# One Trainium2 core, an AdaLN block: the attention product in three fp32r parts, and two steps of VectorE in another order

## What is computed

```python
h = _layernorm(x, axis=-1) * (1 + ca) + sa
# attention
qkv = h @ w_qkv + b_qkv                      # q, k, v: 8 heads of 64
scores = einsum('bhld,bhle->bhde', q, k) / sqrt(64)
attn = softmax(scores, axis=-1)              # 64 x 64 per head
out = einsum('bhld,bhde->bhle', v, attn)     # joined over heads
out = out @ w_fc + b_fc + h
x = x + ga * (_layernorm(out) * gamma + beta)
# channel mix
h = _layernorm(x, axis=-1) * (1 + cb) + sb
h_prev = shift(h, 1)                         # the token before
r = sigmoid((mu_r * h + (1 - mu_r) * h_prev) @ W_r.T)
k = square(relu((mu_k * h + (1 - mu_k) * h_prev) @ W_k.T))
x = x + gb * (r * (k @ W_v.T))
```

## Time and profile before

| | |
|---|---|
| time, median of 3 runs | 690.93 us (690.6 to 691.36) |
| time of the profiled execution | 690.6 us |
| its span | 688.9 us |
| PE busy | 670.7 us (97%) |
| DVE busy | 561.0 us (81%) |
| ACT busy | 393.8 us (57%) |
| POOL busy | 317.5 us (46%) |

### The profile page before, as it was taken

One profiled execution on the slowest core, in us unless ns is written; L12 is line 12 of the kernel. 1 busy time (PEld: TensorE's weight loads), 2 busy tenths in 40 slices (PEclk: granted clock), 3 DMA queues, 4 the chain that ended last, 5 costly groups with the idle time before them and its releaser, 6 DMA issues.

```text
span 688.9 us, 11754 instructions
## 1 busy us (share of the span) xinstructions
PE 670.7 (97%) x3712; PEld 539.4 (78%) x3712; DVE 561.0 (81%) x1254; ACT 393.8 (57%) x871; POOL 317.5 (46%) x520
## 2 busy tenths in 40 slices
PE   7988999999999999999999999999999999999896
PEld 6777886888778887879868887788878788687674
DVE  5693999789887998889887898979988898658973
ACT  1424575566754675474855667546754747547662
POOL 5272864573254642565335742646325753214320
PEclk9989999999999999999999999999999999999999
DMA  8849345485836666572855849366665528628225
GB/s 316 232 152 222 103 131 123 77 212 97 209 74 142 163 135 147 99 167 92 198 113 79 219 91 213 67 141 158 145 136 99 107 72 173 123 37 179 37 31 91
DMA packets 90984, 93.02 MB, mean 135 GB/s; under 512 B 4224, under 2 KB 89000, under 8 KB 90960
## 3 DMA queue, kind: packets, MB, share of 16 engines
q0 software_dynamic: 33264, 33.03, 32.6%
q1 hardware_dynamic: 55344, 55.97, 25.6%
q10 hardware_dynamic: 2352, 3.73, 1.5%
HBM read 42.84 MB, written 33.10 MB: 110 GB/s over the span
## 4 chain that ended last, share of the span: by engine, by line
PE 86%; DVE 7%; POOL 2%; DMA 2%; issue 1%; ACT 1%; SPq 0%; DVEq 0%; POOLq 0%
PE work L1335 14%; PE work L1318 14%; PE att L1285 13%; PE gram L1267 11%; PE gram L1398 4%; PE att L1370 4%; PE work L1151 4%; PE tr L1260 4%; PE work L1153 4%; PE work L1152 4%; PE tr L1302 4%; PE att L1389 2%; PE gram L1380 1%; PE att L1318 1%; DVE st L907 1%
## 5 line engine op out<-in xcount | busy, mean ns | idle before, releaser
L471 POOL TENSOR_TENSOR rs<-ve,neg_half 128x4 f32<-128x4 f32 x32 | 41.6, 1300 | 161.4 <-DVE ve L917 161.4
L1285 PE MATMUL att<-m_sb,z_t 128*128 128x256 f32 x496 | 112.4, 380 | 1.6 <-issue 0.8
L1335 PE MATMUL work<-mx,w_k_t 128*128 128x512 f32 x236 | 106.2, 592 | 0.0
L1285 PEld LDWEIGHTS att<-m_sb,z_t 128*128 128x128 f32 x496 | 92.4, 190 | 16.9 <-issue 5.7
L1318 PE MATMUL work<-w_r_t,mx 128*128 128x256 f32 x464 | 105.7, 381 | 0.0
L1318 PEld LDWEIGHTS work<-w_r_t,mx 128*128 128x128 f32 x464 | 85.9, 190 | 11.1
L1267 PE MATMUL gram<-z 128*128 128x256 f32 (+1 forms) x512 | 90.7, 331 | 0.0
L1267 PEld LDWEIGHTS gram<-z 128*128 128x128 f32 x512 | 81.1, 194 | 6.9
L934 DVE SCALAR_TENSOR_TENSOR mx<-t_buf,mu_col,h2t 128x512 f32<-128x512 f32 x120 | 84.3, 765 | 1.1
L654 ACT ACTIVATE sq<-att 128x256 f32<-128x256 f32 x124 | 46.1, 383 | 64.1 <-PE att L1285 64.1
L1335 PEld LDWEIGHTS work<-mx,w_k_t 128*128 128x128 f32 x236 | 44.8, 190 | 44.1 <-issue 42.6
(11 more groups left out here) (170 smaller groups left out, 1283.6 us busy)
## 6 DMA issues: line engine op xcount, KB each, us to landing
x_in<-in_L_attn_x_dram SPq DMA_DIRECT2D x32, 512.0 KB, 4.8
x<-rows SPq DMA_DIRECT2D x32, 512.0 KB, 3.4
x<-in_L_attn_x_dram POOLq DMA_DIRECT2D x32, 512.0 KB, 8.9
out_dram<-x SPq DMA_DIRECT2D x31, 512.0 KB, 5.1
...
```

The lines of the kernel that those rows point to most:

```text
L1285: ins = mm(att_banks(j, alone)[q][:, (t % 2) * D:(t % 2 + 1) * D], z_t[:, j, k, t * P:(t + 1) * P], m_sb[:, k], start=(k == 0), stop=(k == ...
L1335: ins = mm(k_banks(alone)[dh][:], w_k_t[:, ch, rows_dh], mixed(j, alone)[1][:, ch], start=(ch == 0), stop=(ch == KD - 1))
```

## The change

The attention product becomes three fp32r products for each fp32 one. ACT's copy of the transposed z now writes its high part `z_hi`, and DVE gets a new step `low_z(b, j)` that subtracts it from the transpose in PSUM to give `z_lo`. M gets a high and a low part too, in two more steps of DVE's `make_m`. The next user of tr0 and tr1 now waits for `z_lo_ready` in place of `z_t_ready`, for each bank apart. To make room in SBUF, k's parts lose their second buffer, and the last row's mixed inputs use `mx` rather than `z_t`. In rows 1 to 6 the order of three steps changes: `make_z(n,2)`, `low_k(b-1,3)`, `prep_qk(n)` in place of `prep_qk(n)`, `low_k(b-1,3)`, `make_z(n,2)`.

```diff
-        z_t = sb("z_t", [P, CH, KD, CT])
+        z_hi, z_lo = (part(n, [P, CH, KD, CT]) for n in ("z_hi", "z_lo"))
+        m_hi, m_lo = (part(n, [P, KD, D]) for n in ("m_hi", "m_lo"))
-        k_hi, k_lo = (part(n, [P, 2, KD, CT]) for n in ("k_hi", "k_lo"))
+        k_hi, k_lo = (part(n, [P, KD, CT]) for n in ("k_hi", "k_lo"))
...
+            def low_z(b, j):
+
+                i = CH * b + j
+                for h in range(KD):
+                    dve.wait_ge(z_hi_ready, 2 * i + h + 1)
+                    nc.vector.tensor_tensor(z_lo[:, j, h], tr[h][:], z_hi[:, j, h].bitcast(F32),
+                                            ALU.subtract).then_inc(z_lo_ready, 1)
...
                 nc.vector.tensor_tensor(m_sb[:].rearrange("p k d -> p (k d)"), gram[:],
-                                        res[:].rearrange("p k d -> p (k d)"), ALU.add).then_inc(m_ready, 1)
+                                        res[:].rearrange("p k d -> p (k d)"), ALU.add).then_inc(m_step, 1)
+                dve.wait_ge(m_step, 2 * b + 1)
+                nc.vector.tensor_copy(m_hi[:], m_sb[:]).then_inc(m_step, 1)
+                dve.wait_ge(m_step, 2 * b + 2)
+                nc.vector.tensor_tensor(m_lo[:], m_sb[:], m_hi[:].bitcast(F32), ALU.subtract).then_inc(m_ready, 1)
...
                 take_g(b)
                 prep_now(n)
+                low_z(n, 0)
                 make_x2(b, 0)
                 stats_2(b, 0)
                 if first:
                     stats_a(n, 2)
                     stats_a(n, 3)
+                    low_z(n, 1)
                     make_x2(b, 1)
                     stats_2(b, 1)
                     make_z(n, 2)
                 else:
+                    make_z(n, 2)
+                    low_k(b - 1, 3)
                     prep_qk(n)
-                    low_k(b - 1, 3)
-                    make_z(n, 2)
+                    low_z(n, 1)
                     make_x2(b, 1)
                     stats_2(b, 1)
                 mix(b, 0)
+                low_z(n, 2)
                 if first:
                     prep_qk(n)
                 else:
...
                 mix(b, 1)
+                low_z(n, 3)
                 gate_o(b, 0)
...
                         for k in range(KD):
-                            ins = mm(att_banks(j, alone)[q][:, (t % 2) * D:(t % 2 + 1) * D], z_t[:, j, k, t * P:(t + 1) * P], m_sb[:, k],
-                                     start=(k == 0), stop=(k == KD - 1))
+                            ins = mm3(att_banks(j, alone)[q][:, (t % 2) * D:(t % 2 + 1) * D],
+                                      (z_hi[:, j, k, tile], z_lo[:, j, k, tile], m_hi[:, k], m_lo[:, k]),
+                                      start=(k == 0), stop=(k == KD - 1))
...
-                elif not last and j < CH - 1:
-                    pe.wait_ge(z_t_ready, 2 * (i + 1 + CH) + 2)
...
                 for h in range(KD):
+                    if not last and j < CH - 1:
+                        pe.wait_ge(z_lo_ready, 2 * (i + 1 + CH) + 1 + h)
```

More of the change, by code:

```diff
@@ L162, in y_buf, with k_split, mixed @@
             return x_in[:, j] if alone else y[:, j % 2]
-        def k_split(j):
-            return k_hi[:, j % 2], k_lo[:, j % 2]
+        def k_split(j, alone):
+            return (z_hi[:, 0], z_hi[:, 1]) if alone and j == CH - 1 else (k_hi, k_lo)
         def o_banks(j, alone):
             return att if alone and j == CH - 1 else work[0:2]
-        def mixed(j, alone):
-            return (z_t[:, 2 * j - CH], z_t[:, 2 * j - CH + 1]) if alone and j >= CH // 2 else (xr[:, j % 2], xk[:, j % 2])
+        def mixed(j):
+            return xr[:, j % 2], xk[:, j % 2]
         wmod_sb = h2t[:, :, 1:1 + 6 * D]
@@ L619, in copy_z_t @@
                     act.wait_ge(z_turned, 2 * i + h + 1)
-                    nc.scalar.activation(z_t[:, j, h], tr[h][:], ACT.Copy).then_inc(z_t_ready, 1)
+                    nc.scalar.activation(z_hi[:, j, h], tr[h][:], ACT.Copy).then_inc(z_hi_ready, 1)
             def copy_gram(b):
@@ L685, in take_k @@
                     act.wait_ge(k_sq_ready, 2 * i + h + 1)
-                    nc.scalar.activation(k_split(j)[0][:, h], k[:], ACT.Copy).then_inc(k_hi_ready, 1)
+                    nc.scalar.activation(k_split(j, alone)[0][:, h], k[:], ACT.Copy).then_inc(k_hi_ready, 1)
             def prep_base_qk(b):
@@ L772, in _ @@
             load_more()
[L773 to L774 removed]
+            copy_z_hi(0, 0)
+            copy_z_hi(0, 1)
             act.wait_ge(last_loaded, 16)
@@ L917, in stats_2, with mix @@
                 nc.vector.tensor_scalar(ve_2[:, s], ag_2[:, s, :, 1], EPS_LN, None, ALU.add).then_inc(ve_2_done, 1)
-            def mix(b, j, made=None, alone=False):
+            def mix(b, j, made=None):
                 i = CH * b + j
-                if not alone:
-                    wait_past(dve, r_done, 2 * i - 2)
-                    wait_past(dve, k_done, 2 * i - 2)
+                wait_past(dve, r_done, 2 * i - 2)
+                wait_past(dve, k_done, 2 * i - 2)
                 wait_past(dve, xk_mixed, i)
@@ L931, in mix @@
                 dve.wait_ge(dif_done, i + 1)
-                for n, (dst, ready) in enumerate(zip(mixed(j, alone), (xr_mixed, xk_mixed))):
+                for n, (dst, ready) in enumerate(zip(mixed(j), (xr_mixed, xk_mixed))):
                     for h in range(KD):
@@ L1097, in last_row @@
                 stats_2(b, 3)
-                mix(b, 2, alone=True)
+                mix(b, 2)
                 gate_o(b, 0)
                 low_k(b, 1, alone=True)
-                mix(b, 3, alone=True)
+                mix(b, 3)
                 gate_o(b, 1, alone=True)
@@ L1116, in _ @@
             make_z(0, 1, first=True)
+            low_z(0, 0)
             stats_a(0, 3)
@@ L1120, in _ @@
             prep_now(0)
+            low_z(0, 1)
             make_z(0, 3, first=True)
@@ L1123, in _ @@
             prep_qk(0)
+            low_z(0, 2)
             rows_b()
+            low_z(0, 3)
             centre_fc()
@@ L1249, in turn_and_gram @@
                 pe.wait_ge(z_ready, i + 1)
-                if first or j == 1:
-                    wait_past(pe, z_t_ready, 2 * i)
-                elif j == 0:
+                if j == 0:
                     wait_past(pe, h2_ready, 2 * CH * (b - 1))
-                else:
+                elif not first and j > 1:
                     pe.wait_ge(h2_ready, 2 * (CH * (b - 1) + j - 1))
                 for h in range(KD):
+                    if j > 0 and (first or j == 1):
+                        pe.wait_ge(z_lo_ready, 2 * i - 1 + h)
                     for t in range(NT):
@@ L1317, in ffn_r @@
                         for ch in range(KD):
-                            ins = mm(r_banks(alone)[q][:, (t % 2) * D:(t % 2 + 1) * D], mixed(j, alone)[0][:, ch, tile], w_r_t[:, ch],
+                            ins = mm(r_banks(alone)[q][:, (t % 2) * D:(t % 2 + 1) * D], mixed(j)[0][:, ch, tile], w_r_t[:, ch],
                                      start=(ch == 0), stop=(ch == KD - 1))
```

33 lines of the change are left out of this document (18 added, 15 removed).

## The result

The changed kernel takes 705.21 us (median of 4 runs, 705.17 to 705.49) against 690.91 of the kernel before on the same chip: a ratio of 1.0207, 95% interval 1.019 to 1.0225. It is slower by 14.3 us. The forecast was 706.5. The profiled execution's span is 703.6, 14.7 more than before.

The account below looks back on a forecast made before the run. PE was taken as the bound, busy 670.7 of 688.9 us. Row 0 and start +9.3, rows 1 to 6 +7.8, row 7 -1.0 sum to +16.1, stated as 706.5 us; forecast range 698 to 712.5 (0.66), 8-in-10 range 692 to 713.

Parts of the forecast that it names:

- PE's gain: Attention as three fp32r products on PE: 0.73 us less for each of 32 tiles, 23.4 in all.
- Start of a row: M's two new DVE steps, 1.19 us, cost PE nothing in rows 1 to 6; make_x2(b,0) moves from 7.87 to 9.06.
- Tile 0 to tile 1: DVE's prep_qk and POOL's prep_wv exclude each other at SBUF, so make_x2(b,1) starts at 24.3 against 22.42.
- Four waits: PE gaps before ffn_out(b-1,3), turn_z2(b,0), attention(b,2) and in mid ffn_r(b,0): 4.2 us a row in sum.
- Tile 1 to the next row: Gate's first half at x + 11.1, then 46.1 to the next row: row 81.5, 1.3 longer; six rows +7.8.
- x: Start of make_x2(b,1) counted from attention(b,0): 24.3 us forecast, 22.1 without exclusion, 25.0 from above.
- Row 0 and start: Making M, low_z ahead of PE's work and a slower mix(0,1) add 9.3 us.
- Row 7: DVE sets most of the chain; of attention's 4 x 0.73 gain, 1.0 us is credited (0 to 2.2).
- PE busy down by 20 or more: Sign that would show the prediction right: PE's busy time falls by at least 20.
- (1): Rival: DVE's idle time takes all added work, PE stays the bound; 668.7 us, up to 680; chance 0.12.
- (2): Rival: L991 and L496 do not exclude each other; rows 79.3, total taken as 692 us; chance 0.14.
- (3): Rival: change does what it says but exclusion is worse; x over 25, 713 to 720 us; chance 0.08.

Follow-up runs that it names:

- e3: Changed kernel with POOL's prep_wv(n) moved behind fill_x2(n,0), waiting for mix(b,2), in rows 1 to 6: 694.09 us.
- e4: Changed kernel with low_z(n,2) behind gate_o(b-1,3) instead of ahead of it in rows 1 to 6: 707.05 us.
- e13: Changed kernel with late prep_wv(n) and low_z(n,2), earlier low_k(b-1,3) and low_k(b,0), and ACT making z of tiles 2 and 3 for rows 2 to 7: 684.41 us.
- e1: Changed kernel with the old order prep_qk, low_k(b-1,3), make_z(n,2), then low_z(n,1), in rows 1 to 6: 708.9 us.

## Why the prediction was right, point by point

- **PE's gain.** Forecast 0.73 a tile, measured 399.88 - 396.42 = 3.46 against 2.87 (24 products 0.120 apart), so 0.59. The term was mis-sized: attention's products did not get the spacing of `ffn_out`. Over four tiles of a row it is 0.6. It hardly showed, since three of the four tiles lie where PE waits anyway.
- **Start of a row.** `make_x2(b,0)` forecast at 9.06, measured 392.30 - 383.24 = 9.06. M's parts ready 0.57 ahead: 381.98 + 0.69 = 382.67, 0.57 before `attention`.
- **Tile 0 to tile 1.** `make_z` forecast at 14.16 for 1.3: 14.20 and 1.38. `low_k` done at 16.74: 16.78. `make_x2(b,1)` forecast at 24.3, with the exclusion as its reason: 24.09. e3 confirmed the reason by taking it away (22.2).
- **Four waits.** Forecast 4.2 in sum: 3.8 by the spacing of starts, 2.8 by the idle times. The first was set at 0.95, where its own terms give 0.90 (16.74 - 15.84), and is 0.72, since `attention` was taken as too short.
- **Tile 1 to the next row.** Second half of `ffn_r(b,0)` forecast at x + 11.1: 418.39 - 407.33 = 11.06. Row 81.5: 81.48. That this is so exact is luck: x came 0.2 earlier than forecast, and from that half to the next row it took 46.3 instead of 46.1, as `attention(b,3)` gave less. The statement that nothing else stalls was true with a slack of under 1 us at `ffn_out(b,0)`; e4 showed how near it was.
- **Row 0 and start.** Forecast +9.3, measured 7.9 for `attention(1,0)` (131.04 to 138.93). `turn_z2(0,2)` forecast at 108.2, or 109.1 with the 0.9 for the first softmax, measured 107.61. `mix(0,1)` was given 4.84 + 2 and took 6.36. The 0.9 was too much, M comes 0.4 later. And neg_d, which waits for a DMA, came 1.1 later (64.92 against 63.81), where the forecast had it 1.2 + 0.9 later. The forecast also left falls of PE's clock out of its sum, without a reason. The one at 68.81, 3.4 us at half the clock, could have cost 1.7 (an estimate from its length) had waits not taken it up, which again is luck.
- **Row 7.** Forecast -1.0, measured -0.7. That one was a choice between 0 and 2.2, not a walk.
- **PE busy down by 20 or more** was wrong: 9.1. Of four tiles at 0.59, 2.4 us a row, about 1 is hidden in records that reach into a wait (3.8 lost, 2.8 seen as idle), and row 0 ran at a lower clock for longer.
- **The rivals.** (1), PE stays the bound, wanted x = 20.1. Even e3 has 22.2. (In e13 PE is the bound at x = 21.4 to 21.5, but with `low_z(n,2)`, 1.2 us, behind the gate.) (2), no exclusion, is refuted by the 2.65 of L1001. Its row of 79.3 is near what e3 shows without the exclusion, 79.6. (3) did not occur; x stayed under 25.

```profile
107.61 1.16 PE L1327 MATMUL tr<-ident,z 128*128 128x128 f32 x8 [2.90 <-DVE z_lo L945]
```

This is the line for `turn_z2(0,2)` against the earlier trace rows, which stood at 99.85 without a wait. In rows 1 to 6 the forecasts of single times held to about 0.2 us, and e1 to e4 bear out the mechanism, so there the walk along both engines was sound. For row 0 and the start it was coarser, and the total, right to 1.3, leans on errors that partly cancel. Its sum, 16.1 against 14.7, erred by 1.4 at the start and in row 0 together and by 0.3 in the rows; row 7 gave 0.3 less than forecast.
